# Moving the skip term and one clip bound from VectorE to GpSimd in a language-model layer, with list scatters split over two turns

## What is computed

```
scale = max(|w|)/127 per table row;  q = clip(round(w/scale), -127, 127) * scale;  h = q[ids]
x = layernorm(h)
z, xBC, dt = x @ in_proj.T ;  xBC = silu(conv4(xBC) + b) ;  x, B, C = split(xBC)     # x is 384 wide
y = ssd(x*dt, dt*A, B, C) + D*x          # per sequence of 128 tokens: (C B^T * decay) @ (x dt), plus the skip term D*x
y = rmsnorm(y * silu(z)) * norm_w ;  h = h + layernorm(h) + sigmoid(g) * (y @ out_proj.T)
n = layernorm(h) ; two routers (softmax, argmax over 4 experts each)
h = h + n_common_expert(...) + dropped * n_unique_expert(...)     # dropped: tokens beyond the 2048 best of an expert
```

## Time and profile before

| | |
|---|---|
| time, median of 3 runs | 1050.79 us |
| lowest, highest | 1050.75, 2953.04 us |
| profiled execution, its span | 1055.1 us (no other time of that execution is given) |
| busy over the span | PE 921.0 us (87%), DVE 680.5 (64%), ACT 584.7 (55%), POOL 531.7 (50%) |
| mean granted TensorE clock | 0.964 |
| chain that ended last, by engine | PE 43%, DVE 24%, ACT 13%, issue 11%, POOL 4%, DMA 3% |
| DVE L1445 (convolution) | 231 operations, 168.4 us, mean 740 ns |
| DVE L1478 (`y`) | 192 operations, 333 to 348 ns each |
| POOL L520 (`gate_y`) | 64 operations, 68.5 us, mean 1070 ns |

### The profile page before, as it was taken

One profiled execution on the slowest core, in us unless ns is written; L12 is line 12 of the kernel. 1 busy time (PEld: TensorE's weight loads), 2 busy tenths in 40 slices (PEclk: granted clock), 3 DMA queues, 4 the chain that ended last, 5 costly groups with the idle time before them and its releaser, 6 DMA issues.

```text
span 1055.1 us, 19890 instructions
## 1 busy us (share of the span) xinstructions
PE 921.0 (87%) x5743; PEld 603.5 (57%) x5744; DVE 680.5 (64%) x1999; ACT 584.7 (55%) x1196; POOL 531.7 (50%) x638
## 2 busy tenths in 40 slices
PE   0677899899998998989988889899998999999986
PEld 0233455455554554555645667677766767677764
DVE  3778999999998999999988433666671121222120
ACT  3667887788878877888765344232322332323320
POOL 6332445456455555462432446334337777775552
PEclk9899999999999999999997789999998999999997
DMA  4920011011101111010002121124332121213220
GB/s 109 319 59 8 16 46 43 5 46 49 46 18 32 46 48 37 12 47 30 33 2 84 42 64 51 52 86 141 97 90 60 53 66 49 70 49 86 62 59 19
DMA packets 50001, 61.54 MB, mean 58 GB/s; under 512 B 22524, under 2 KB 41688, under 8 KB 49412
## 3 DMA queue, kind: packets, MB, share of 16 engines
q0 software_dynamic: 16704, 30.54, 10.3%
q1 hardware_dynamic: 28580, 24.93, 7.8%
q10 hardware_dynamic: 4640, 5.13, 1.7%
HBM read 36.24 MB, written 25.92 MB: 59 GB/s over the span
## 4 chain that ended last, share of the span: by engine, by line
PE 43%; DVE 24%; ACT 13%; issue 11%; POOL 4%; DMA 3%; DVEq 0%; POOLq 0%; ACTq 0%
DVE xbc L1445 10%; PE cx L1232 6%; PE yb L1232 6%; PE mm L1075 5%; PE mm L1220 4%; PE mm L1216 4%; PE mm L1079 3%; PE sg L1216 3%; DMA xg<-hr_dram,ids 3%; PE tp L1043 2%; DVE mix L1465 2%; POOL list_u L585 2%; ACT rows_s L757 2%; PE sg L993 2%; ACT h L704 2%
## 5 line engine op out<-in xcount | busy, mean ns | idle before, releaser
L1445 DVE SCALAR_TENSOR_TENSOR xbc<-mm,cw,xbc 128x508 f32<-128x508 f32 (+2 forms) x231 | 168.4, 740 | 18.1 <-ACT xbc L732 12.5
L1075 PE MATMUL mm<-xt_a,win_a 128*128 128x512 f32 x248 | 139.3, 644 | 36.1 <-DVE xbc L1445 24.2
L914 ACT ACTIVATE ht<-mm,b1s 128x256 f32<-128x256 f32 x102 | 44.7, 472 | 221.8 <-PE sg L1220 219.2
L601 POOL DMA_INDIRECT xg<-hr_dram,ids x80 | 81.2, 1015 | 88.0 <-DVE res L1780 43.8
L520 POOL TENSOR_TENSOR ybuf<-ybuf,zs 128x384 f32<-128x384 f32 x64 | 68.5, 1070 | 99.6 <-DVE ybuf L1478 99.4
L620 POOL DMA_INDIRECT out_dram<-osb,ids_s x80 | 82.3, 1029 | 66.9 <-DVE osb L1790 47.6
L732 ACT ACTIVATE xbc<-mm,cb,cw 128x512 f32<-128x512 f32 x77 | 56.6, 775 | 100.1 <-PE mm L1079 100.1
L1790 DVE TENSOR_TENSOR osb<-cx,res 128x192 f32<-128x192 f32 x40 | 14.2, 356 | 129.8 <-PE cx L1232 128.0
L1216 PE MATMUL mm<-fx_a,w1a_t 128*128 128x256 f32 x240 | 81.0, 420 | 8.1 <-issue 7.6
L1220 PE MATMUL mm<-fx_b,w1b_t 64*128 64x256 f32 x240 | 85.0, 435 | 0.0
L1220 PE MATMUL sg<-fx_b,w1b_t 64*128 64x256 f32 x240 | 85.0, 435 | 0.0
(11 more groups left out here) (275 smaller groups left out, 2062.6 us busy)
## 6 DMA issues: line engine op xcount, KB each, us to landing
hr_dram<-hr SPq DMA_DIRECT2D x16, 768.0 KB
w2s<-in_w2c_dram SPq DMA_DIRECT2D x4, 576.0 KB
w2s_u<-in_w2u_dram ACTq DMA_DIRECT2D x4, 576.0 KB
list_c<-fill SPq DMA_DIRECT2D x2, 1032.0 KB, 12.8
list_u<-fill SPq DMA_DIRECT2D x2, 1032.0 KB, 19.2
w1a<-in_w1c_dram SPq DMA_DIRECT2D x4, 384.0 KB
w1a_u<-in_w1u_dram ACTq DMA_DIRECT2D x4, 384.0 KB
xg<-hr_dram,ids POOLq DMA_INDIRECT x80, 3.1
```

Of the source, the lines that this page charges most:

```text
L601: nc.gpsimd.indirect_dma_start(out=xg[:, v, t, :], out_offset=None, in_=rows, in_offset=bass.IndirectOffsetOnAxis(ap=ids[:, v, t, 0:1], ax ...
L1075: mmul(tile_bank(g2, m)[:, :], win_a[:, column(m):column(m) + P], xt_a[:, p, :], start=True, stop=False)
L1445: ins = stt(out=dst_[:, :, back:L], in0=src[:, :, 0:L - back], scalar=cw[:, m, TAPS - 1 - back:TAPS - back], in1=dst_[:, :, back:L], op0=A ...
```

## The change

VectorE's `y(j)` becomes one addition of 128x384, `ybuf = yb + ybuf`. The product `dskip * xbc` is written to `ybuf` beforehand by GpSimd (`skip_terms`): three operations of 128x512 a turn, for the group that the next turn scans, once ScalarE's SiLU is done (`s_xbc`) and the output products that read this buffer are done (`s_o`). VectorE's `y(0)` waits for them (`s_skip`) in place of its wait for `s_o`.

VectorE's `clip` is split into `cap` (subtract MAGIC, `min` with 127), now ahead of `stats2`, and `stats1` (the row statistics) in its old place. The `max` with -127 is GpSimd's `clip_low`, between the two; `stats1` waits for it (`s_clip`).

The gathers take their ids from `xids` in place; the copy to `gidx` and the wait for it are gone. `list_tokens(1)` of a batch runs in the next turn, behind `gate_y(0)`, so that four scatters are issued in each turn.

```
-STEPS = dict(norm=3, quant=2, clip=3, ...)
+STEPS = dict(norm=3, quant=2, clip=1, ...)
 # GpSimd
             def gather(g):
                 wait(pool, s_rd, g - 1)
-                nc.gpsimd.tensor_copy(gidx[:, p, :], xids[:, GS * g:GS * (g + 1)]).then_inc(s_idx, 1)
-                pool.wait_ge(s_idx, g + 1)
                 for j in range(GS):
                     nc.gpsimd.indirect_dma_start(
                         ...
-                        in_offset=bass.IndirectOffsetOnAxis(ap=gidx[:, p, j:j + 1], axis=0)).then_inc(s_gath[p], 16)
+                        in_offset=bass.IndirectOffsetOnAxis(ap=xids[:, GS * g + j:GS * g + j + 1], axis=0)).then_inc(s_gath[p], 16)
+            def clip_low(g):
+                pool.wait_ge(s_cap, g + 1)
+                nc.gpsimd.tensor_scalar(h0[:, :, :], h0[:, :, :], -QMAX, None, ALU.max).then_inc(s_clip, 1)
+                def skip_terms():
+                    if g2 is None:
+                        return
+                    p = g2 % 2
+                    wait(pool, s_o, 2 * (g2 - 1))
+                    pool.wait_ge(s_xbc, g2 + 1)
+                    for c in range(ZT):
+                        last = nc.gpsimd.tensor_scalar(ybuf[:, p, c, :], xbc[:, p, c, :], dskip[:, c:c + 1], None, ALU.mult)
+                    last.then_inc(s_skip, 1)
                 def list_tokens(part=None):
-                    of, g = listed_turn(t)
+                    of, g = listed_turn(t - 1 if part == 1 else t)
                 if t == LAST_SSD:
                     ...
+                    list_tokens(1)
                     list_tokens()
                     return
                 gate_y(0)
                 list_tokens(0)
+                list_tokens(1)
                 rms()
                 gate_y(1)
                 if t + 2 < NG:
                     gather(t + 2)
                 gate_y(2)
+                skip_terms()
+                if t + 1 < NG:
+                    clip_low(t + 1)
                 norm2()
-                list_tokens(1)
                 gate_y(3)
                 ...
             # before the turns: clip_low(0) ahead of norm1(0)
 # VectorE
-            def clip(g):
-                p, link = g % 2, Chain(dve, ch["clip"], g, STEPS["clip"])
+            def cap(g):
                 dve.wait_ge(s_rd, g + 1)
-                link(ts(h0[:, :, :], h0[:, :, :], MAGIC, QMAX, ALU.subtract, ALU.min))
-                link(ts(h0[:, :, :], h0[:, :, :], -QMAX, None, ALU.max))
+                ts(h0[:, :, :], h0[:, :, :], MAGIC, QMAX, ALU.subtract, ALU.min).then_inc(s_cap, 1)
+            def stats1(g):
+                link = Chain(dve, ch["clip"], g, STEPS["clip"])
+                dve.wait_ge(s_clip, g + 1)
                 wait(dve, s_rs1, g)
                 row_stats(lambda j: h0[:, j, :], st1, mv1, link).then_inc(s_ve, 1)
                 def y(j):
                     if j == 0:
-                        wait(dve, s_o, 2 * (g3 - 1))
+                        dve.wait_ge(s_skip, g3 + 1)
                     dve.wait_ge(s_yp, GS * g3 + j + 1)
-                    for c in range(ZT):
-                        last = stt(out=ybuf[:, p, c, js], in0=xbc[:, p, c, js], scalar=dskip[:, c:c + 1],
-                                   in1=yb[:, c * P:(c + 1) * P], op0=ALU.mult, op1=ALU.add)
-                    last.then_inc(s_yd, 1)
+                    tt(ybuf[:, p, :, js], yb[:, 0:ZT * P].rearrange("p (c l) -> p c l", c=ZT), ybuf[:, p, :, js],
+                       ALU.add).then_inc(s_yd, 1)
                 pick()
+                if t + 1 < NG:
+                    cap(t + 1)
                 stats2()
                 y(3)
                 if t + 1 < NG:
-                    clip(t + 1)
+                    stats1(t + 1)
```

More of the change, by code:

```diff
@@ L73 @@
 ROWS = 32
-STEPS = dict(norm=3, quant=2, clip=3, tap=10, soft=9, ssd=4, h1=2, pick1=1, pick2=6, place=2, find=6)
+STEPS = dict(norm=3, quant=2, clip=1, tap=10, soft=9, ssd=4, h1=2, pick1=1, pick2=6, place=2, find=6)
 def wait(eng, sem, value):
@@ L219, in build @@
         side_c, side_s = sb("side_c", [P, 2], c=a), sb("side_s", [P, P], c=a)
-        gidx = sb("gidx", [P, 2, GS], I32, c=a)
         hx = sb("hx", [P, 4, GS, D], c=a)
@@ L279, in build @@
         s_const, s_prep, s_pe_, s_sig = sem("constants"), sem("prepared"), sem("exp_a_log"), sem("exp_gate")
-        s_idx, s_q, s_rd = sem("gather_index"), sem("quant_scale"), sem("rounded")
+        s_q, s_rd = sem("quant_scale"), sem("rounded")
+        s_cap, s_clip, s_skip = sem("capped"), sem("clipped"), sem("skip_terms")
         s_gath = [sem(f"gathered{p}") for p in range(2)]
@@ L642, in _ @@
             nc.gpsimd.memset(zrow[:, :], 0.0)
+            clip_low(0)
             norm1(0)
@@ L1367, in _ @@
             quantise(0)
-            clip(0)
+            cap(0)
+            stats1(0)
             dve.wait_ge(s_sig, 1)
```

## The result

| | median, lowest to highest | runs | ratio to before, 95% interval |
|---|---|---|---|
| kernel before, beside it | 1052.14, 1050.58 to 2953.04 us | 20 | |
| changed kernel | 1059.41, 1054.68 to 1064.13 us | 20 | 1.0057 [1.004, 1.0074] |
| changed kernel, on another chip | 1056.38, 1052.78 to 1066.95 us | 12 | 1.003 [1.0006, 1.0054] |

The ratios leave out two outliers of the kernel before (1189.50 and 2953.04 us) and are not quotients of the medians. By them the changed kernel is slower by 3 to 6 us, where 4.2 us less were forecast, and both medians lie outside the range. That it would stay within 2% held. The profiled execution took 1063.15 us. Turns are numbered as before: turn 10 starts at its first convolution and ends with that of turn 11.

The account below looks back on a forecast made before the run. VectorE was taken to be full in stage A only, ScalarE's chain limiting turn ends. Even tails 2.4, odd turns 1.1, start 0.4 and stage A's end 0.3 made 4.2 us saved: 1046.6 us, range 1041.5 to 1054.5.

Parts of the forecast that it names:

- The step that failed: Price of GpSimd's new operations, from memset plus affine_select's extra: 0.68 us a skip operation, 0.97 us for clip_low.
- The wait that I excluded: stats1 waiting for clip_low at a turn's end: none claimed, since 2.2 us of stats2 and y(3) lie between.
- my high bound: Highest price of GpSimd's new operations, scaled from two-input gate_y: 1.32 us a skip operation, 1.98 us for clip_low.
- it is wrong ... if `stats1` waits: Sign against the forecast: VectorE's row statistics at a turn's end waiting for GpSimd; no such wait was expected.
- The stall of `pick`: In even turns, pick's two-input VectorE operations wait for GpSimd's skip operations: 1.1 us a turn.
- The alternation: VectorE's two-input operations and GpSimd's operations take turns, each VectorE one waiting at most for the GpSimd operation under way.
- The floor 1.0 us below an even turn: At an even turn's end at most 1.0 us can be gained, since ScalarE's chain to the next convolution comes next.
- the 0.4 us at the start: Before the turns, the first clip ends at 16.1 us in place of 16.5: 0.4 us saved.
- the 0.4 forecast for a turn's tail: Behind an even turn's last convolution: 1.5 us saved (y 0.9, clip 0.59) less a 1.1 us stall; 0.4 us left.
- 0.18: us saved in an odd turn's first half, where y(1) waits for VectorE; shortening above 0.2 us would show the forecast wrong.
- GpSimd blocks more than it saves: Rival, chance 0.17: at 1.32 us a skip operation, pick's waits total 2.3 us an even turn; slower, +4.0, 1055 us.
- the clock rival: Rival, chance 0.05: stage A ending elsewhere moves TensorE's lower-clock stretches; a slice at 1.2 GHz worth some 10 us either way.

Follow-up runs that it names:

- x1: Changed kernel with the whole clip back on VectorE at the turn's end, skip terms still on GpSimd: 1049.28 us, ratio 0.9965 to the kernel before.
- x2: Changed kernel with y in three VectorE operations and no skip terms on GpSimd; clip_low stays there: 1054.67 us, ratio 1.0007 to the kernel before.
- x4: Changed kernel with clip_low ahead of skip_terms in GpSimd's order: 1052.98 us, ratio 0.9986 to the kernel before.
- x3: Only four scatters a turn and ids read in place; clip and y as in the kernel before: 1052.51 us, ratio 0.9985.
- x10: The changed kernel itself once more, beside its variants, on another chip: 1056.38 us, ratio 1.003 to the kernel before.
- x16: The kernel before, unchanged, run and profiled once more: 1052.14 us, ratio 0.9983.
- x9: The best order: changed kernel with clip_low ahead of the skip terms and the first clip, before the turns, wholly on VectorE: 1055.53 us, ratio 1.0005.
- x13: Same kernel as x9 (clip_low first, first clip on VectorE), run a second time: 1051.31 us, ratio 0.9959 to the kernel before.
- x14: Same kernel as x9 (clip_low first, first clip on VectorE), run a third time: 1050.94 us, ratio 0.9967 to the kernel before.
- x5: Same kernel as x9, on the chip about 7% slower: 1125.15 us, ratio 1.0025 to the kernel before, which took 1122.86 us there.
- x11: Same kernel as x1 (whole clip on VectorE, skip terms on GpSimd), once more: 1052.2 us, ratio 0.9985 to the kernel before.
- x12: Changed kernel with only its first clip, before the turns, wholly on VectorE; clip_low stays behind the skip terms: 1062.0 us, ratio 1.0078.
- x15: Same kernel as x12 (only the first clip on VectorE), once more: 1057.48 us, ratio 1.0016 to the kernel before.

## Why the prediction was wrong

**The step that failed** is "Low bound, the memset of 384 columns ... so I take 0.59 + 0.09 = 0.68 us", with the bound above it and the same for `clip_low`. The trace had no wide tensor_scalar on GpSimd, and I bounded it above by a wide operation with two inputs. It is slower than that: 1.55 us for 512 columns is 3.0 ns a column, 2.14 for 768 is 2.8, where `gate_y` takes 2.6. Fewer inputs did not make it cheaper, and neither a memset nor a select resembles it. The Trainium skill ("GPSIMD Engine Reference", "3.1 Elementwise — side-by-side cycle accounting") gives its 769 ns for 512 elements as the best case of a software loop; the trace shows twice that.

**The wait that I excluded** followed from the size and from the order of the queue. I set the 2.2 us between `cap` and `stats1` against `clip_low`'s own duration, at most 1.98, and did not ask what GpSimd would still be doing when `cap` ends. In an even turn it would have been idle even at my high bound: 362.55 + 3 x 1.32 = 366.5, before 366.83. At the measured 5.7 us it is busy until 368.25, and 368.33 + 2.15 = 370.48 is past 369.64. In an odd turn the step fails even within my bounds: there `cap` ends at 399.64, at my high bound the skip operations of turn 11 end at 396.95 + 3.96 = 400.9, and with 1.98 for `clip_low` `stats1`, free at 402.3, would wait 0.6 us. I had written that "it is wrong ... if `stats1` waits"; it does in 13 turns. x1, x2 and x4 show that this wait is the loss inside the turns: without it, at the same price of each operation, the pair is 1.3 to 1.7 us shorter.

I also left out that VectorE holds up GpSimd. In turn 10 the three skip operations took 2.27, 1.56 and 1.90 us, the first beside `mix`, the third beside `cap`; behind `clip_low` in x4 they took 4.65 us together in place of 5.71.

**The stall of `pick`** was oversized. In x1, with skip operations of 1.55 to 2.27 us beside it, `oh` takes 0.49 us in place of 0.22, and two copies 0.32 and 0.25 in place of 0.17 each. These overlap, and `pick` as a whole is 0.3 us longer. The forecast was 1.1 at less than half that price, and 2.3 for the rival. Two-input operations of VectorE did not wait for the end of GpSimd's: `oh` in turn 10 of the changed kernel ended at 365.56, the skip operation beside it ran from 364.81 to 366.37, and in x4 a `mix` that began 0.7 us into a skip operation took 0.95 us, its free duration. Operations with one input vary: `minus` of turn 10 ended at 369.19 and `clip_low`, begun at 368.33, at 370.48, while in x4 `var` ended with `clip_low` (364.48). The alternation that I built the sum on was seen beside `gate_y` and a copy and did not carry over.

**What held.** `y` at 0.55 us. The floor 1.0 us below an even turn, set by ScalarE's tile: x4 and its kin reached it exactly. Lists and ids worth nothing inside the turns; the 0.4 us at the start did not show (x3: 32.17 us, the kernel before 31.37 to 31.88). x1's even turn is 0.56 us shorter, near the 0.4 forecast for a turn's tail, but by luck: x1 has only `y`'s 0.9 us of the 1.5, and by the forecast's stall of 1.1 it would have gained nothing. 0.9 less the 0.3 measured is what it got. x1's odd turn is 0.27 us shorter, where I had 0.18 and called more than 0.2 a sign of being wrong.

**The rivals.** The one that ends slower, "GpSimd blocks more than it saves", named the right engine and nearly the time (1055), but its mechanism was the stall of `pick`, which is small. The right one was the second half of the same engine's queue. Of the clock rival there is a part: see below.

**The sum as measured**, up to the start of turn 16, the changed kernel's second profile (x10) against the first of before: start 33.04 in place of 31.88, +1.2; the six even turns from 4 to 14 +0.3 to +0.5 each, 2.1 together; the odd turns from 3 to 15 +1.8; turns 1 and 2 cancel. In all 542.4 against 537.4 us: +5.0. Forecast were -0.4 for the start, -2.4 and -1.1. From there to the end of stage A, where I had -0.3, this profile gains 3.5 us at a granted clock of 0.88 against 0.80, which leaves +1.5 (against x16, -0.6). The first profile of the changed kernel stood at 549.2 at turn 16: turn 2 took 2.3 us and turn 15 4.2 us more than in the profile of before, at clocks of 0.90 and 0.87. That is clock, and most of it was not there in its second profile; at the end of stage A it was 9.4 us behind. So the later start and the longer turns at full clock stand in both profiles, and how much of them is left in the whole, +3.2 or +6.0 us by the ratios, goes with the clock. The second stage, which is not touched, took 451.8 to 457.6 us in the profiles, 457.6 and 451.8 for the kernel before itself.

**Where the best order's gain went.** Pairs 1.0 us shorter should give some 6 us. x9, x13 and x14 are one kernel: ratios 1.0005, 0.9959 and 0.9967, weighted by their runs 0.998, or 2 us (x5, the same kernel on the slower chip, had 1.0025). In x13 turns 9, 12 and 13 at the lower clock cost 1.7 + 0.8 + 3.9 = 6.4 us over their full-clock lengths; the kernel before lost 0.5 in its turn 7 and up to 0.7 in turn 9. So in that profile the gain inside the turns was given back as clock: turn 16 of x13 starts at 538.6 us, against 537.4 and 539.3 in the two profiles of before. At the end of stage A it is 2.4 to 4.4 us ahead of them. The skip terms alone (x1, x11: 0.9965 and 0.9985) do no worse, with a simpler queue; it is the version that I would keep, and its gain, 1.6 to 3.7 us, is at the edge of what these runs resolve.

## What to carry to other kernels

Before work is moved to an idle engine, lay out its queue from the last operation ahead to the first consumer, with the highest price and more. Here two moves that each paid became a loss together, since the one that was waited for stood last. Put the operation that someone waits for ahead of the one that is needed a turn later; here that swap alone was worth 1.7 us a pair of turns. A bound from another kind of operation is not a bound; where the trace has no row of the kind, leave room above the highest. And lay it out for every kind of turn: the one with less work ahead of the consumer, not the fullest one, waited longest here.

## What the runs showed of the hardware

- A wide float32 tensor_scalar on GpSimd takes 2.8 to 3.0 ns a column (1.55 us for 128x512, 2.13 for 128x768), with a constant 1.48 us for 512: slower per column than a product of two tensors (0.99 us for 384).
- VectorE and GpSimd held each other up for parts of an operation, both ways. A skip operation begun beside `mix` took 2.27 us in place of 1.55. `oh`, with two SBUF inputs, took 0.49 in place of 0.22 when it began 0.3 us into a skip operation; a `mix` begun 0.7 us into one took its free 0.95.
- Shorter turns were not shorter time in full: TensorE's lower level (1.2 GHz) took 6.4 us from three turns of x13. In x12, x15 and in turns 12 and 13 of x9, x13, x14 the drops came again in the same turns; in turns 12 and 13 of x4, whose turns have the same program, they did not, and between x1 and x11 only turns 10 and 15 were low in both.
- One chip ran all kernels 7% slower (1122.86 against 1052 us for the kernel before), at a granted clock of 0.93 to 0.95 against 0.95 to 0.97 on the chip of x1 to x4, with pauses in TensorE's stream. Times were comparable only within a set.
